# Last stage of an audio tower: softmax ahead of the chunk norm, the norm through another PSUM bank

## The reference

```
h = h + L0_ffn(...)                         # rows of the first experts, times each token's gate
x = layernorm(h)                            # norm "e"
q, k, v = x @ qkv_w.T + qkv_b
attn = softmax(q . k[7 neighbours] + rpb)   # 16 heads, window of 7 positions
h = h + (sum_o attn_o * v_o) @ proj_w.T + proj_b
x = layernorm(h)                            # norm "f"
logits = mean_over_sequence(x) @ router_w.T # 11 partitions of 6, top 2, -> weights of 6 experts
out = h + sum_e w_e * (gelu(x @ W1[e] + b1[e]) @ W2[e] + b2[e])
```

## Time and profile before

| what | us |
|---|---|
| median of 3 runs | 921.07 (918.88 to 927.0) |
| profiled execution, its own time | 919.01 |
| its span, first to last instruction | 917.2 |
| last stage within the span | about 591 to 917 |
| steady period at full clock (727 to 762) | 34.9 |

### The profile page before, as it was taken

One profiled execution on the slowest core, in us unless ns is written; L12 is line 12 of the kernel. 1 busy time (PEld: TensorE's weight loads), 2 busy tenths in 40 slices (PEclk: granted clock), 3 DMA queues, 4 the chain that ended last, 5 costly groups with the idle time before them and its releaser, 6 DMA issues.

```text
span 917.2 us, 11017 instructions
## 1 busy us (share of the span) xinstructions
PE 623.7 (68%) x2992; PEld 467.0 (51%) x2993; DVE 687.2 (75%) x1433; ACT 491.0 (54%) x709; POOL 326.1 (36%) x314
## 2 busy tenths in 40 slices
PE   6983453834627438276651599356998989989896
PEld 3552353834626438253441377323765756666664
DVE  0888287999999999996863244378889889788752
ACT  1143999899999898931330133143445445355442
POOL 0344101313313134131387144313545456354432
PEclk9995677868768678698755699766999999899998
DMA  4380004365345543514311112110000000000000
GB/s 165 122 282 1 1 0 84 76 107 98 66 81 110 95 77 66 100 32 162 112 27 33 32 58 58 52 38 1 0 1 9 1 9 9 0 9 9 1 9 17
DMA packets 22521, 50.65 MB, mean 55 GB/s; under 512 B 4610, under 2 KB 14955, under 8 KB 22128
## 3 DMA queue, kind: packets, MB, share of 16 engines
q0 software_dynamic: 6752, 24.53, 14.3%
q1 hardware_dynamic: 15728, 25.64, 8.7%
HBM read 24.13 MB, written 10.10 MB: 37 GB/s over the span
## 4 chain that ended last, share of the span: by engine, by line
PE 43%; DVE 20%; issue 12%; ACT 8%; POOL 7%; DMA 5%; POOLq 3%; DVEq 0%; ACTq 0%; SPq 0%
PE psum L1808 9%; PE psum L1564 5%; DVE s_xs L237 4%; DMA s_xnfm<-s_R 3%; PE psum L1735 3%; POOLq L178 3%; PE psum L1748 3%; DVE s_R L1092 3%; PE psum L1800 2%; DVE s_R L1079 2%; POOL s_part L616 2%; PE psum L1825 2%; POOL s_mean L620 2%; PE psum L1626 2%; PE psum L1627 2%
## 5 line engine op out<-in xcount | busy, mean ns | idle before, releaser
L1626 PE MATMUL psum<-s_xn_lo,s_split_hi 128*128 128x368 f32 x256 | 95.7, 374 | 143.2 <-ACT s_R L823 138.7
L1626 PEld LDWEIGHTS psum<-s_xn_lo,s_split_hi 128*128 128x128 f32 x256 | 55.2, 216 | 148.0 <-ACT s_R L823 141.4
L1808 PE MATMUL psum<-s_R 128*128 128x368 f32 (+1 forms) x288 | 105.6, 495 | 1.2 <-ACT s_R L926 1.2
L1098 DVE TENSOR_TENSOR_SCAN s_R<-s_R 128x2944 f32<-128x2944 f32 x16 | 100.7, 6291 | 0.8
L1627 PE MATMUL psum<-s_xn_hi,s_split_lo 128*128 128x368 f32 x256 | 92.3, 361 | 0.0
L1628 PE MATMUL psum<-s_xn_hi,s_split_hi 128*128 128x368 f32 x256 | 92.0, 359 | 0.0
L926 ACT ACTIVATE s_R<-psum,s_cols 128x368 f32<-128x368 f32 x96 | 50.7, 567 | 73.7 <-PE psum L1802 73.7
L707 POOL TENSOR_TENSOR s_R<-s_R 128x368 f32<-128x368 f32 x48 | 47.1, 982 | 76.2 <-DVE s_R L1494 75.6
L683 POOL TENSOR_TENSOR s_R<-s_R 128x368 f32<-128x368 f32 x48 | 45.8, 953 | 67.9 <-DVE s_R L1383 46.3
L1808 PEld LDWEIGHTS psum<-s_R 128*128 128x128 f32 (+1 forms) x288 | 53.5, 197 | 26.0 <-issue 6.1
L830 ACT ACTIVATE s_R<-psum,s_cols 128x736 f32<-128x736 f32 x64 | 55.9, 877 | 16.3 <-PE psum L1628 11.9
(11 more groups left out here) (221 smaller groups left out, 1621.3 us busy)
## 6 DMA issues: line engine op xcount, KB each, us to landing
s_xnfm<-s_R POOLq DMA_DIRECT2D x14, 1472.0 KB, 10.5
s_R<-in_xg SPq DMA_DIRECT2D x8, 744.0 KB, 4.2
x_sorted<-in_x_init SPq DMA_DIRECT2D x1, 5082.0 KB, 18.5
s_R<-in_w SPq DMA_DIRECT2D x2, 1536.0 KB, 7.9
s_wBC<-in_wBC SPq DMA_DIRECT2D x8, 256.0 KB, 2.7
s_R<-x_sorted SPq DMA_DIRECT2D x28, 66.0 KB, 1.8
s_R<-y_rows SPq DMA_DIRECT2D x8, 184.0 KB
out<-s_R SPq DMA_DIRECT2D x8, 184.0 KB
```

The source lines that it names most:

```text
L1098: dve.tensor_tensor_scan(bufB[:, u], ra[:, u], bufB[:, u], 0.0, ALU.mult, ALU.add).then_inc(ra_free, 1)
L1626: pe.matmul(bank(c), w_hi[:, s, u, k, :], xn_lo[:, a:b], start=True, stop=False)
L1808: ins = pe.matmul(bank((2, 4)[e % 2]), w, fh[0:kk, e % 3, j], start=(j == 0), stop=(j == FT - 1))
```

## The change

1. `shares` on DVE moves ahead of `normed_f`; `shares_rest` moves ahead of `split_stream`, and `stream_sums` and the weighing of expert 4 move behind the first offset.
2. On PE `shares_fm` moves ahead of norm f's transposes, which now stand behind two of expert 5's three second-layer steps, and go to bank 5 in place of bank 7. The router's logits move behind the second spread and two first-layer steps. On ACT `shares_out` moves ahead of norm f's copies.
3. Bank 7 no longer holds norm f, so the second spread waits for `store_chunk` (`out_ready`) and no longer for the copies.
4. POOL adds the bias of chunk `c - 1` at the head of period `c`, no longer that of chunk `c` in the middle of period `c`.
5. `first_experts` is four instructions of 128 columns, each multiply and add, in place of two of 512 columns.
6. `router_largest` has one small instruction less, and the one that takes off the maximum now reads PSUM.

```diff
--- before.py
+++ after.py
@@ POOL, head of a period
                 add_expert(c - 3, 5)
+                if 1 <= c <= NCH:
+                    projection_bias(c - 1)
                 if c + 1 < NCH:
                     rstd_e(c + 1)
...
                 add_expert(c - 2, 3)
-                if c < NCH:
-                    projection_bias(c)
                 add_expert(c - 2, 4)
@@ ACT
                 gelus(c - 2, 27, 33)
-                if 1 <= c <= NCH:
-                    norm_copies(act, nF, (c - 1) % 2, c - 1, (7, 7), dst=xnfm, hi=xn_hi)
                 if c < NCH:
                     shares_out(c)
+                if 1 <= c <= NCH:
+                    norm_copies(act, nF, (c - 1) % 2, c - 1, (5, 5), dst=xnfm, hi=xn_hi)
@@ DVE, first_experts
-                g = gate[:, c * CB:(c + 1) * CB].rearrange("p (j o) -> p j o", o=1).to_broadcast([L, CB, D])
-                step.add(dve.tensor_tensor(seqs(OG, c), seqs(OG, c), g, ALU.mult))
-                step.wait()
-                step.add(dve.tensor_tensor(seqs(H, c), seqs(H, c), seqs(OG, c), ALU.add))
+                for j in range(c * CB, (c + 1) * CB):
+                    step.add(dve.scalar_tensor_tensor(H[:, j, :], OG[:, j, :], gate[:, j:j + 1], H[:, j, :],
+                                                      ALU.mult, ALU.add))
@@ DVE, router_largest
-                ts(zz[0], psum[0:CB, 5, 448:448 + NPART], 1.0 / L, None, ALU.mult)
-                red(s1[0], zz[0], ALU.max)
-                ts(zz[0], zz[0], s1[0], None, ALU.subtract)
+                sums = psum[0:CB, 5, 448:448 + NPART]
+                red(s1[0], sums, ALU.max)
+                ts(zz[0], sums, s1[0], 1.0 / L, ALU.subtract, ALU.mult)
@@ DVE, middle of a period
                 weigh_expert(f - 1, 3)
+                if att:
+                    shares(c)
                 if tail:
                     normed_f(f)
                 if att:
-                    shares(c)
+                    shares_rest(c)
                 if tail:
                     split_stream(f)
-                if att:
-                    shares_rest(c)
-                if tail:
-                    stream_sums(f)
-                weigh_expert(f - 1, 4)
                 for o in range(K):
                     if att:
                         offset(c, o)
+                    if o == 0:
+                        if tail:
+                            stream_sums(f)
+                        weigh_expert(f - 1, 4)
@@ PE, result_tm and spread_out
                 pe.wait_ge(facc_add, g * NE + NE + 2)
+                if g:
+                    pe.wait_ge(out_ready, g)
...
                 elif o == 1:
-                    if c:
-                        pe.wait_ge(nF.xT_free, c + 2)
+                    if c >= 3:
+                        pe.wait_ge(out_ready, c - 2)
@@ PE, middle of a period
-                if tail:
-                    if c >= 3:
-                        pe.wait_ge(out_ready, c - 2)
-                    norm_transposes(pe, nF, f % 2, f, (7, 7))
                 if att:
                     shares_fm(c)
-                ffn(f - 1, 33, 34)
+                ffn(f - 1, 33, 35)
+                if tail:
+                    norm_transposes(pe, nF, f % 2, f, (5, 5))
...
                     if o == 0:
-                        ffn(f - 1, 34, NF)
-                        if tail:
-                            router_logits(f)
+                        ffn(f - 1, 35, NF)
                     else:
                         ffn(f, 2 * o - 2, 2 * o)
+                    if o == 1 and tail:
+                        router_logits(f)
```

More of the change, by code:

```diff
@@ L1931, in _ @@
                 ffn(f, 15, 18)
-            pe.wait_ge(out_ready, NCH - 1)
             result_tm(NCH - 1)
```

## The result

The changed kernel takes 904.22 us (median of 4 runs, 902.75 to 904.76), the kernel before 920.0 us (median of 4, 918.88 to 927.0): a ratio of 0.9835, 95% interval 0.9806 to 0.9864. The forecast was 902 us, in a range of 895 to 911. The span of the profiled execution went from 917.2 to 902.4 us, 14.8 us less.

What follows compares the result with a forecast made beforehand. PE and DVE were both near full (31.9 and 31.2 us busy a period), so their waits for each other counted. From 919.0 us, 12.3 for six periods, 0.6 for period 1 and 4 for the clock gave 902 us, range 895 to 911.

Steps and rivals of the forecast that it cites:

- The largest term: Six periods with the sixth spread starting earlier: 2.05 us each, 12.3 us; bounds 1.25 to 2.66 us a period.
- Shares first: DVE makes shares before the norm: PE's 1.82 us wait goes, first spread starts 1.6 us earlier.
- The norm without the bias: DVE's four norm instructions, no longer beside POOL's bias, take 1.78 us in place of 2.72.
- The wait in front of the low part of the norm: DVE idles some 1.4 us for ACT's copies, losing 0.3 of the 1.6 us; `normed_e` starts 1.27 us earlier.
- The router: DVE's maximum subtraction reads PSUM, one instruction goes: about 0.6 plus 0.15 us saved a period.
- Gated sum and bias at the head: Start of the period: counted as zero, DVE waiting for PE anyway; bias might cost up to 0.3 us a period.
- The clock: PE's clock falls less as its waits shrink: 4 of 5.4 us won, bounds 0 and 5.4.
- The ends: Period 1 gains the router's 0.6 us; period 8 zero, give or take 0.6; period 9 untouched.
- the wait only moves: Rival: ACT's copies come later or POOL still hits the router; 1.25 us a period stay, 909 us, chance 0.10.
- the clock would fall as before: Rival: PE waits of a few tenths still drop the clock; only 12.9 us stay, 906 us, chance 0.14.
- deeper: Rival: PE loses its whole 2.66 us six times and the clock never falls, 897 us, chance 0.13.
- the third: The third rival, "the wait only moves": 909 us, chance 0.10.

Runs made afterwards that it cites:

- e5b: Changed kernel with expert 4's weighing and the first offset moved on DVE ahead of the low part of the norm: 898.67 us, ratio 0.9791.
- e6b: Changed kernel with two of the router's 4 x 11 temporaries put in unused columns of PSUM bank 5: 900.33 us, ratio 0.9809.
- e8b: Kernel before with only POOL's bias moved to the head of the period: 907.94 us, ratio 0.9893.
- e2: Kernel before with bias at the head, four-instruction gated sum and router change, in the old order of shares and norm: 908.24 us, ratio 0.9897.
- e1: Changed kernel with bias, gated sum and router put back as before, keeping the new order and bank 5: 903.15 us, ratio 0.9861.
- e9: Changed kernel with the edits of e5b and e6b, and PE in period 8 transposing the norm before expert 5's two steps: 897.83 us, ratio 0.9786.
- e3: Changed kernel with POOL's bias back in the middle of the period: 903.04 us, ratio 0.9851.
- e7b: Changed kernel with the edits of e5b and e6b together: 898.65 us, ratio 0.9789.

## Why the prediction was right, point by point

The time and its main mechanism were right; the sum was 16.9 us against 14.8 us measured between the two spans. That the total came this close is in part luck. The largest term, 12.3 us for six periods, was about twice what came at full clock (6 x 1.05 = 6.3 us), and steady periods took 33.8 us where 32.6 to 33.0 were forecast. It was made up for by 7.3 us more from the four periods whose clock had fallen, where 4 were forecast, and by 2.4 us ahead of period 2, where 0.6 were; period 8 took 1.1 us back. The parts, in the order of the prediction:

- **Shares first:** right. The 1.82 us wait went, and the first spread came 1.71 us earlier (1.6 forecast).
- **The norm without the bias:** right in direction, too small: 1.10 us, not 1.78. The row that I took for "without POOL" (`normed_e`, 750.47 to 752.25 in the earlier trace rows) had itself a POOL add beside it. The surplus was lost in the wait for ACT.
- **The wait in front of the low part of the norm:** right in place, 1.92 us against 1.4. `normed_e` started 1.21 us earlier (1.27 forecast). e5b shows that this wait was the part of the change most worth mending.
- **The router, the step that failed:** 0.75 us forecast, 0.19 measured. The prediction let the next instruction with two SBUF operands wait for the same add, but took the length of the wait as saved. That instruction is the very next one, and it waits until the add ends. The add ends 1.13 us behind the router's start in both kernels (753.88 and 752.75 before, 745.93 and 744.80 after), and nothing behind that point can start sooner: what was saved is the one instruction less that stands behind it. e6b shows the wait gone when the operands leave SBUF.
- **`normed_e`, not foreseen:** 0.33 us longer, because expert 4's weighing moved behind the first offset, and POOL's add for it now abuts the first add of the offsets. With the 0.56 us that the router did not give, it makes nearly all of the difference between 2.05 us forecast and 1.05 measured. From the start of `normed_e` to the fourth offset it is 4.51 us, 0.14 more than before, where the forecast had 0.75 less.
- **Gated sum and bias at the head:** zero, right: DVE's way to the weighing of expert 3 is 13.33 us before and after. The sizes are now measured: 1.12 us for four instructions with POOL idle, where the estimate from the columns was 1.1; 1.68 us beside the bias. The old shape beside the bias would have cost 0.15 us a period (e8b).
- **The two halves as a sum:** the prediction took the bias as a detail of the norm's length. e8b and e2 show that the bias alone shortens the steady period by 0.8 us, and the rest without the order by 1.16, as much as the whole. What the order gives beyond that is, as far as the profiles go, a steady clock: none of the kernels with the new order shows a fall, e2 shows two, and e8b's one profile, of its fastest run, none. On the same chip e1 took 903.15 us and e2 908.24.
- **The clock:** 4 us forecast, too small; no steady period of the profile has a fall. The periods 2, 3 and 5 came down by 2.06, 2.65 and 3.32 us, those at full clock (4 and 6) by 1.06 and 1.04; so the falls were worth 1.0, 1.6 and 2.3 us there, and some of period 7's 3.45. The prediction counted period 7 as 0.6 us above 34.8, but this period has less for DVE to do and takes 32.8 us at full clock in e8b, whose edit gave 0.8 us elsewhere. By that its fall was worth some 1.7 us (an estimate from these numbers), and all of them together 6.6, above the bound of 5.4.
- **The ends:** period 8 cost 1.14 us, where 0 with a margin of 0.6 was forecast; e9 shows why. Up to the end of period 1, 2.36 us were won where 0.6 were forecast. The changed kernel's three profiles end period 1 at 652.5, 655.1 and 652.8, a spread as large as this gain, so these runs do not tell how much of it is the change's.

The rival "the wait only moves" happened in part: POOL hit the router all the same, and the wait for ACT was longer. Its price of 1.25 us a period was near the truth (1.05), and its 909 us were wrong mainly because of the clock. That the clock would fall as before did not come about with the new order; with e2 it fell in two periods of six.

One slip in the chances: "forecast, deeper, clock and most of the third" come to 0.87 without the third, so 0.88 with most of its 0.10 is too low by some 0.06.

## What to carry to other kernels

When two edits shorten the same path, price each alone and then ask what bounds the loop with both: here one gave 0.87 and the other 1.16 us a period, and together they gave 1.05. Before moving an instruction's operand to take away a stall, look down the row for the next instruction with the same need: it inherits the wait. And after a reorder, look for the wait that it made in front of a late result and put work that is ready there: that gave more here (1.3 us a period) than the reorder itself.

## What the runs showed of the hardware

- A DVE instruction on 4 x 11 numbers takes 0.15 to 0.22 us, and up to 1.17 us when POOL is in an add: it ends 0.01 to 0.04 us after POOL does. It was seen with two operands in SBUF, and for a subtraction or comparison from SBUF to SBUF with one scalar; with the tensor operand in PSUM, 0.17 us were measured beside the same add.
- A longer one waits too and then does its work: the last instruction of the shares (92 x 448, two operands in SBUF) takes 0.93 us alone and 1.60 us beside the bias in e3, and ends 0.78 us after it.
- POOL waits in the same way. Its 92 x 4 instruction of 0.19 us takes 3.24 us when it starts just as DVE begins seven multiplications that run without a gap for 3.08 us, and ends with them. POOL's row in the changed kernel, its wait ahead of it in brackets:

```profile
724.95 3.24 POOL L226 TENSOR_SCALAR s_pa<-s_mv 92x4 f32<-92x4 f32 x1 [2.34 <-DVE s_mv L206]
```

DVE's row of the seven, in the same kernel:

```profile
725.07 3.08 DVE L1405 TENSOR_TENSOR s_R<-s_R 128x344 f32<-128x344 f32 x7
```

- TensorE's clock fell from 2.4 to 1.2 GHz in four of six periods in which PE waited 1.8 and 0.5 us shortly one after the other (before), and in two of six with 1.1 and 0.5 us (e2), each time within 0.6 us behind one of these two waits. With 1.1 and 0.5 us it did not fall in the profile of e8b. It fell in none with one wait of 1.09 us and no other above 0.42 (e1), and in none with waits of at most 0.9 us (the change, e3, e5b, e6b, e7b, e9). What decides whether it falls in a given period was not settled.
